# A fused attention and expert layer: routing steps and weight maxima moved on VectorE

## The reference

```
x = x + attention(layernorm(x))            # 16 heads, causal, softmax
xf = layernorm(x)                          # 8192 x 256
xn = layernorm(xf) * ln_scale + ln_bias
probs = softmax(xn @ gate_w.T)             # 8 experts
tk_probs, tk_idx = top_k(probs, 2)
tk_probs = tk_probs / (sum(tk_probs) + 1e-5)
w[:, e] = the weight with which a token goes to expert e
out = swiglu(xf, sWg, sWu, sWd)            # the shared expert, all tokens
for e in range(8):
    out = out + w[:, e:e+1] * swiglu(xf, Wg[e], Wu[e], Wd[e])
x = x + out                                # swiglu: (silu(x @ wg) * (x @ wu)) @ wd, 256 -> 512 -> 256
```

## Time and profile before

| | us |
|---|---|
| median of 3 runs | 1657.58 (1655.62 to 1658.88) |
| the profiled execution | 1656.44 |
| its span | 1654.7 |
| PE busy | 1513.6 (91%) |
| VectorE busy | 1054.2 (64%) |
| ScalarE busy | 828.8 (50%) |
| POOL busy | 898.4 (54%) |
| mean granted clock of TensorE | 0.972 |

### The profile page before, as it was taken

One profiled execution on the slowest core, in us unless ns is written; L12 is line 12 of the kernel. 1 busy time (PEld: TensorE's weight loads), 2 busy tenths in 40 slices (PEclk: granted clock), 3 DMA queues, 4 the chain that ended last, 5 costly groups with the idle time before them and its releaser, 6 DMA issues.

```text
span 1654.7 us, 41571 instructions
## 1 busy us (share of the span) xinstructions
PE 1513.6 (91%) x14714; PEld 1103.3 (67%) x14716; DVE 1054.2 (64%) x1852; ACT 828.8 (50%) x1252; POOL 898.4 (54%) x1121
## 2 busy tenths in 40 slices
PE   3689999999999999987698989999999999999995
PEld 2345555555555555543586778888888898888884
DVE  7567888887888888877478777753333333333332
ACT  1266767666666666656132225544444444444442
POOL 2144555554555555544123667736766666666663
PEclk9699999999999999999699999999999999999998
DMA  2323333333233333243866854446766666666563
GB/s 83 96 91 90 116 100 113 103 109 111 90 110 111 109 108 112 91 126 94 185 176 178 194 122 98 107 107 94 109 103 98 100 100 103 99 101 100 100 102 37
DMA packets 283156, 181.03 MB, mean 109 GB/s; under 512 B 160625, under 2 KB 273649, under 8 KB 282962
## 3 DMA queue, kind: packets, MB, share of 16 engines
q1 hardware_dynamic: 244370, 130.25, 30.9%
q0 software_dynamic: 30016, 35.55, 14.6%
q10 hardware_dynamic: 8576, 12.58, 2.4%
HBM read 83.91 MB, written 60.17 MB: 87 GB/s over the span
## 4 chain that ended last, share of the span: by engine, by line
PE 67%; DVE 10%; DMA 8%; SPq 5%; issue 3%; ACT 3%; POOL 3%; DVEq 0%; POOLq 0%; ACTq 0%
PE bank L1574 20%; PE pair_s L1848 13%; PE bank L1709 7%; PE bank L1848 6%; PE pair_t L1848 6%; PE pair_s L1636 4%; SPq L441 3%; PE bank L1744 3%; PE pair_t L1683 3%; DMA qk_d<-qkl 2%; ACT prob L882 2%; DVE early L1501 1%; POOL prob L684 1%; PE pair_s L1656 1%; ACT early L991 1%
## 5 line engine op out<-in xcount | busy, mean ns | idle before, releaser
L882 ACT ACTIVATE prob<-pair_t 128x1024 f32<-128x1024 f32 x320 | 327.4, 1023 | 233.3 <-PE pair_t L1683 228.4
L684 POOL TENSOR_SCALAR_AFFINE_SELECT prob<-prob 128x256 f32<-128x256 f32 (+1 forms) x448 | 198.4, 456 | 334.0 <-ACT prob L882 329.3
L807 POOL DMA_INDIRECT out_x<-ysb,tok_rows x135 | 217.6, 1612 | 158.6 <-ACT ysb L1018 105.2
L991 ACT CAST early<-early 128x512 f16<-128x512 f32 (+1 forms) x206 | 124.3, 603 | 333.6 <-DVE early L1501 333.6
L1507 DVE TENSOR_TENSOR early<-early 128x512 f16<-128x512 f32 (+1 forms) x206 | 139.1, 675 | 137.9 <-ACT early L991 137.3
L1501 DVE SCALAR_TENSOR_TENSOR early<-pair_s,h_s,sg 128x512 f32<-128x512 f32 (+1 forms) x103 | 75.3, 731 | 225.4 <-PE pair_s L1848 223.2
L766 POOL DMA_INDIRECT tok_d<-tok_w,dest_i x128 | 137.1, 1071 | 103.9 <-DVE dest_i L1426 52.8
L1574 PE MATMUL bank<-wbuf,early 128*128 x1620 | 188.7, 273 | 4.6 <-DVE early L1507 2.8
L1848 PE MATMUL pair_s<-xt,wbuf 128*128 128x256 f16 x1704 | 188.7, 267 | 0.0
L1709 PE MATMUL bank<-prob,v_op 128*32 128x512 f32 (+3 forms) x2048 | 179.1, 445 | 5.1 <-POOL prob L684 5.0
L1157 DVE TENSOR_REDUCE mx<-pair_s 128x2 f32<-128x1024 f32 x128 | 156.8, 1225 | 41.1 <-PE pair_s L1656 40.3
(11 more groups left out here) (273 smaller groups left out, 2742.8 us busy)
## 6 DMA issues: line engine op xcount, KB each, us to landing
q_op<-qk_d SPq DMA_DIRECT2D x192, 64.0 KB, 2.6
k_op<-qk_d SPq DMA_DIRECT2D x192, 64.0 KB, 2.7
x_in<-in_L_attn_x SPq DMA_DIRECT2D x16, 512.0 KB, 3.9
qk_d<-qkh SPq DMA_DIRECT2D x32, 256.0 KB, 2.2
qk_d<-qkl SPq DMA_DIRECT2D x32, 256.0 KB, 2.6
xres<-in_L_attn_x SPq DMA_DIRECT2D x16, 512.0 KB, 4.6
x_d<-x SPq DMA_DIRECT2D x32, 256.0 KB, 2.2
xhl_d<-xhl SPq DMA_DIRECT2D x32, 256.0 KB, 2.5
```

What stands on the lines that cost most here:

```text
L684: last = nc.gpsimd.affine_select(out=v, in_=v, compare_op=ALU.is_ge, fill=0.0, base=0, pattern=[[0, v.shape[1]], [1, P]], channel_multipli ...
L807: pool.indirect_dma_start(out=out, out_offset=bass.IndirectOffsetOnAxis(ap=tok_rows[:, block, 0:1], axis=0), in_=ysb[:, here], in_offset=N ...
L882: nc.scalar.activation(prob[:, half, u].rearrange("p a n -> p (a n)"), pair_t[:].rearrange("p a n -> p (a n)"), ACT.Exp, scale=exp_by).the ...
L991: nc.scalar.copy(hth2[:, par, 2 * hh:2 * hh + 2, 0:w], hb2[:, hh, 0:2 * w].rearrange("p (c n) -> p c n", c=2)).then_inc(S["hh_done"], 1)
```

## The change

The maxima get a tile of their own, `tops`, with a column for each matrix and expert. `first` is one instruction that counts up `wmax_done` itself; the join to `run3` and the two links go. A new step, `all_first`, behind the maxima of unit 15, waits for all 24 and reduces `tops` to `run3`; PE then waits for 25 in place of 24. The first of the three maxima of a unit (k = 0) runs between the halves, the other two behind the results, ahead of the stages of `AFTER`.

The steps of the routing move. Unit 2 keeps `one_hot(0)`; `largest(1)` goes between the halves of unit 3 and `one_hot(1)` behind it; `choose` goes between the halves of unit 4 and `count` behind it; `weigh` goes between the halves of unit 5 and `count_blocks` behind it; `rows_in_order` goes behind unit 6, `place` behind unit 7 and `experts_of_units` behind unit 16. All other queues stay.

```diff
+        tops = sb("tops", [P, 3, E], F32)
...
-                nc.vector.memset(run3[:], 0.0)
...
-                link.link(dve, nc.vector.tensor_reduce(
-                    top[:, 0, k:k + 1], wraw[:, e + 1, off // 2:off // 2 + n], AX_X, ALU.max,
-                    apply_absolute_value=True))
-                link.link(dve, nc.vector.tensor_tensor(run3[:, k:k + 1], run3[:, k:k + 1], top[:, 0, k:k + 1],
-                                                       ALU.max))
-                nc.vector.sem_inc(S["wmax_done"], 1)
+                nc.vector.tensor_reduce(tops[:, k, e:e + 1], wraw[:, e + 1, off // 2:off // 2 + n], AX_X, ALU.max,
+                                        apply_absolute_value=True).then_inc(S["wmax_done"], 1)
+
+            def all_first():
+
+                dve.wait_ge(S["wmax_done"], 3 * E)
+                nc.vector.tensor_reduce(run3[:], tops[:], AX_X, ALU.max).then_inc(S["wmax_done"], 1)
...
-            AFTER = {0: (deviations,), 1: (route_logits, lambda: largest(0, lg)), 2: (lambda: one_hot(0), lambda: largest(1, lg2)),
-                     3: (lambda: one_hot(1), choose), 4: (count, count_blocks), 5: (weigh, rows_in_order),
-                     6: (place, experts_of_units)}
+            AFTER = {0: (deviations,), 1: (route_logits, lambda: largest(0, lg)), 2: (lambda: one_hot(0),),
+                     3: (lambda: one_hot(1),), 4: (count,), 5: (count_blocks,), 6: (rows_in_order,), 7: (place,),
+                     FIRST_AT + E - 1: (all_first,), FIRST_AT + E: (experts_of_units,)}
+            BETWEEN = {3: (lambda: largest(1, lg2),), 4: (choose,), 5: (weigh,)}
...
                 unit_low(u, u % 2, 0, 2 * P)
+                for stage in BETWEEN.get(u, ()):
+                    stage()
+                for e, k in expert_parts(u, FIRST_AT, 3):
+                    if k == 0:
+                        first(e, k)
                 unit_hidden(u, 1, 2 * P, 1)
...
+                for e, k in expert_parts(u, FIRST_AT, 3):
+                    if k > 0:
+                        first(e, k)
                 for stage in AFTER.get(u, ()):
                     stage()
-                for e, k in expert_parts(u, FIRST_AT, 3):
-                    first(e, k)
...
-                    pe.wait_ge(S["wmax_done"], 3 * E)
+                    pe.wait_ge(S["wmax_done"], 3 * E + 1)
```

## The result

| | before | after |
|---|---|---|
| first comparison, median | 1656.69 us (1655.62 to 1658.88, 4 runs) | 1640.39 us (1638.13 to 1642.63, 4 runs) |
| ratio | | 0.9909, 95% interval 0.9893 to 0.9925 |
| all runs of this study together, median | 1654.9 us (86 runs) | 1641.7 us (21 runs) |
| profiled execution, its span | 1656.44, 1654.7 | 1641.40, 1639.7 |
| PE, VectorE, POOL busy | 1513.6, 1054.2, 898.4 | 1506.1, 1045.2, 895.8 |

The change makes the kernel faster by 13.2 us on all runs (1654.9 - 1641.7).

The account below looks back on a forecast made before the run. VectorE was taken to bound the shared units up to 16, with about 19 us of PE idle. PE ready 12.8 us earlier, less 2.1 idle and 0.5 clock, wins 10.2: 1657.58 - 10.2 = 1647.4 us, range 1644 to 1653.5.

Parts of the forecast that it names:

- H(5): Start of VectorE's first product of shared unit 5; forecast at 868.6, set by ScalarE's silu.
- H(8): Start of VectorE's first product of shared unit 8, where the maxima begin; forecast at 896.6.
- H(16): Start of VectorE's first product of shared unit 16, after the maxima; forecast at 963.5.
- (a): Joins removed in units 8 to 15: 24 maxima at 1.14 us instead of 1.59, 10.9 us less VectorE work.
- (b): Routing steps moved: no gain before unit 8 by spreading; `experts_of_units`, 4.25 us, leaves the queue ahead of the last maximum.
- (c): Maxima in units 8 to 15: VectorE's unit 8.33 us, PE's unit 18 beginning 12.8 us earlier.
- rival E: Maxima keep a 1.25 us pitch; win 10 us or little less; chance 0.63 together with forecast A.
- (d): POOL's scatters: first one 5.3 us later, end at 1076.2, only 4.3 us earlier, so routed columns come late.
- forecast A: The scatters end the chain before PE's routed part; 10.2 us won; chance 0.63 together with rival E.
- The chain behind them: From the last scatter's end through `tok_rows` read, gathers and transposes to PE's routed columns: 12.8 us.
- the 0.5 us for the clock: Slower PE products after its 2.1 us idle for the routed columns, put at 0.5 us.
- rival B: Scatters hidden anyway, by short landings or a 1.278 pitch; all 12.8 us won, 1644.8; chance 0.14.

Follow-up runs that it names:

- e1: The kernel before, run once more unchanged under a name of its own; ratio 0.9995 (0.9979 to 1.0011).
- e2: The kernel before with only the tile `tops` added and left unused; ratio 1.0 (0.9986 to 1.0014).
- e4: The kernel before with only the routing steps moved as in the change, old maxima and joins kept; ratio 0.9997 (0.998 to 1.0013).

## Why the prediction came out too high

**Right: PE and VectorE.** Predicted instants, turned to "from unit 1", against the first profile after:

| step | predicted | measured |
|---|---|---|
| pitch of two maxima | 1.14 | 1.13 |
| H(5) | 43.35 | 43.49 |
| H(8) | 71.35 | 71.45 |
| H(16) | 138.25 | 137.55 |
| PE's unit 18 | 148.15 | 147.60 |
| PE's wait for `sel` | 1.8 | 1.67 |
| PE ready for the columns | 261.65 | 261.05 to 261.47 (repeats) |

Edit by edit (a), (b) and (c) of the prediction hold within 0.7 us; rival E is out by the pitch. It is also right that the routing steps alone give back nothing, and more so than I thought. Together with the maxima they bring 264.01 to 261.4, 2.6 us: the transpose of `run3` comes 4.0 us earlier (138.14 in the first repeat, 142.14 with the maxima alone), and the wait for the peak behind `experts_of_units` takes 1.3 of them back, this time with no slow products behind it.

**Wrong: the end of the scatters, (d).** The forecast A had the last scatter end at 250.95 and the columns 12.8 us behind it at 263.75, so that PE loses 2.1 + 0.5 us.

- The first scatter (72.35 predicted, 72.47 measured) and the pitch of the first 60 (1.31; 1.32 in the first profile, 1.30 in the repeats) were right. The last 68 were sized at 98.8 + 1.2 = 100.0 us. They took 97.2 in the first profile and 97.0 to 97.2 in the repeats, 1.43 each (in the first profile POOL is busy 1.116 us a scatter in place of the 1.153 of the earlier trace rows). The count was right: before, 22 of the 24 low halves start ahead of the end of the last scatter, and now all 24. But the 1.2 us for the two more did not show, and the 98.8 of one execution were themselves open: the kernel before, run again, has 97.6 for the same 68. The end came at 248.84 and, in the repeats, at 247.4 to 248.0.
- The chain behind them was sized at 12.8 and is 11.7 in the one kernel that has PE wait for it alone; the difference lies behind the first gather, where gather, landings and transposes were put at 8.6 and take 7.5. It was 13.3 in the first profile, by the 4.75 in place of 3.0 us ahead of the first gather.
- No run shows the 0.5 us for the clock behind a wait of 2.1 us: where the clock fell behind waits of 1.80 to 4.46 us it cost 1.7, and behind others of 2.09 to 3.19 it did not fall (last section). A's lower end, 6.7 us with the worst landings, leaves this 0.5 out; with it the sum is 6.2.

With 247.7 + 11.7 = 259.4 the columns are 2.0 us early, not 2.1 late. That is rival B, which I gave 0.14, though by the last 68 and the chain and not by a pitch of 1.278 in the first 60. The 2.1 us between the two were less than what the terms may be off by together: the pitch of the first 60 alone was open by 1.9 us in the prediction itself. A and B deserved like chances. B's win was put at 12.8; the three repeats have 13.1, 12.7 and 13.4. The first profile met the forecast's 10.2 with 10.8 because of two waits of PE that the repeats do not have or have only in part: 0.89 us for the columns and 1.38 for ScalarE's silu, which the prediction had priced at 1 if its cover failed. So the nearness of 10.8 to 10.2 is luck.

**Wrong: the base and the range.** I took 10.2 from 1657.58, the median of three runs. The 86 runs have a median of 1654.9 and go from 1648 to 1664. That alone puts the forecast 2.7 us too high; 3.0 more are the shared part (13.2 - 10.2). The sum, 5.7, is the distance from 1647.4 to 1641.7, and the first four runs happened to lie another 1.3 lower. In the first pair of profiles 15.0 us separate the executions and only 10.8 of them are in the shared part; 4.2 are in attention, where the change does nothing but drop a memset. Unit 1 of PE starts, in executions that have the same attention:

| kernels | start of unit 1, us |
|---|---|
| before and its near copies (e1, e2, e4) | 825.25, 824.79, 823.80, 823.06 |
| the change (first, then repeats) | 821.08, 823.18, 825.62, 824.82 |
| other variants | 818.16 to 826.87 |

So this is scatter, 8.7 us wide, and no effect of the change shows in it. The clock is an obvious suspect: the windows 300 to 350 and 400 to 450 of attention have 0.97 in the profile before, and after they have:

```profile
300.00:350.00 50.00, 47.18 (x493) 25.56 (x491) 41.52 (x81) 32.86 (x46) 27.21 (x48) 1.00 0.35 107
400.00:450.00 50.00, 47.81 (x497) 26.01 (x498) 42.00 (x80) 33.55 (x48) 26.52 (x49) 1.00 0.35 105
```

But these windows do not go with the start of unit 1: the first repeat has 0.97 in both and starts it at 823.18, the second has 1.00 in both and starts it at 825.62, and the kernel before, run again, has 1.00 in both and 824.79. What makes attention longer in one execution than in another stays open. A range for the kernel's time has to carry this scatter besides the doubts of the sum; mine ended at B's time on the unlucky base, 1644.0, with nothing below it.

**Half settled: what sets the end now.** I add the idle times that PE's timeline prints from unit 1 to the first routed product, and what its products took beyond 1.31 us per 12. That gives 23.3 us before (274.48), 14.7 with the maxima alone (264.01), 10.2 in the change (261.38), 11.4 and 9.5 with two maxima a unit (261.27 and 259.86). Less that sum each is 251.2, 249.3, 251.2, 249.9 and 250.4, and the routing steps alone (22.3 and 274.49) leave 252.2. So the waits explain the instants within 1.5 us; the timeline does not print the shortest waits, and I have not found the rest.

## What to carry to other kernels

Where an engine sets the pace and each small step of it waits for its own forerunner, look at the time from start to start: write the results to places of their own and join them once, or a step late. Before a chain is called the new bound, write its end beside the next bound's: when they lie closer than the sum of the terms' errors, both are forecasts, and the range goes by both. And take the base from as many runs as there are, or add the scatter of one run to the range.

## What the runs showed of the hardware

- Behind a wait of PE its clock falls or stays, and the length of the wait alone does not decide which. After idle stretches of 1.62 and 1.67 us the next products ran at full speed. After 1.80, 2.10, 2.12, 3.09, 3.73 and 4.46 us they were slow by 1.7 us altogether, whatever the stretch; after 6.32 and 7.26 us by 2.5. But the kernel before, run again, waits as long at the same places and loses nothing there:

```profile
871.82 1.48 PE L1848 MATMUL pair_s<-xrow,wsh 128*128 128x256 f16 x12 [2.09 <-DVE early L1501]
...
895.80 1.49 PE L1848 MATMUL pair_s<-xrow,wsh 128*128 128x256 f16 x12 [3.19 <-DVE early L1501]
```

  It does lose 1.7 us behind a wait of 2.66 us between the two, and the kernel with the unused tile shows the same three (2.11 and 3.18 without loss, 2.66 with it). So a wait of 2 to 3 us can cost 1.7 us more or nothing. The prediction read 0.94 behind the 2.10 us of the earlier trace rows, from the first block of 12; the block behind that one was slow by another 0.78 (2.25 in place of 1.47).
- An instruction of VectorE on 128x1 costs 0.06 us from start to start when what it reads is long done, and 0.30 with 0.12 more in front of it when each waits for the one before.
- The 128 scatters of POOL have a pitch of 1.30 us before the low halves of the weights begin and 1.44 beside them (67 and 61 of them in the repeats). With the low halves packed three a unit, from a later unit on, 43 lie beside them at 1.41, and the last 68 have 1.37 on average.
